# A copy moved into two number chains of VectorE, and gate matmuls cut to the chunks that are read

## The reference

```
# attention: 32 heads of 8, chunks of 32 tokens
gate = einsum('bshd,bnhd->bhsn', q, kmean)       # token against the mean key of each chunk
gate = where(future, NEG, gate); gate = where(self_blk, -NEG, gate)
sel  = top-4 chunks of each token and head
p    = softmax(where(sel & causal, q @ k.T * scale, NEG));  o = p @ v
rms  = rsqrt(mean(o * o) + EPS);  o = o * rms * o_norm_weight * sigmoid(g)
x    = layernorm(x + o @ Wo.T)
# experts: 2 shared, 16 routed with top-4 gates, 176 wide, relu
x    = layernorm(x + flat + shared + routed)
```

## Time and profile before

| | us |
|---|---|
| median of three runs | 1547.78 (1541.15 to 1549.93) |
| the profiled execution, its own time | 1541.77 |
| its span in the trace | 1539.7 |
| TensorE busy | 1373.1 (89%) |
| VectorE busy | 1170.6 (76%) |
| ScalarE busy | 845.4 (55%) |
| GpSimd busy | 550.0 (36%) |
| mean granted clock of TensorE | 0.958 of full |

### The profile page before, as it was taken

One profiled execution on the slowest core, in us unless ns is written; L12 is line 12 of the kernel. 1 busy time (PEld: TensorE's weight loads), 2 busy tenths in 40 slices (PEclk: granted clock), 3 DMA queues, 4 the chain that ended last, 5 costly groups with the idle time before them and its releaser, 6 DMA issues.

```text
span 1539.7 us, 29870 instructions
## 1 busy us (share of the span) xinstructions
PE 1373.1 (89%) x11220; PEld 756.7 (49%) x11220; DVE 1170.6 (76%) x2931; ACT 845.4 (55%) x1266; POOL 550.0 (36%) x638
## 2 busy tenths in 40 slices
PE   5587999999998899989999899989999899998697
PEld 3322565526653366534654266543664346552364
DVE  7993789867897688967898678976889668885534
ACT  5407663395625766286643956357662776438221
POOL 4204442254323442254322543235422443225143
PEclk8757999999999999999999999999999999999798
DMA  6001022200221021210122002210112102220031
GB/s 242 8 7 16 29 71 66 45 29 20 83 66 43 15 57 63 67 24 29 63 70 50 17 28 83 65 46 17 50 62 69 30 15 59 72 52 15 14 105 61
DMA packets 52212, 77.85 MB, mean 51 GB/s; under 512 B 6322, under 2 KB 26724, under 8 KB 51812
## 3 DMA queue, kind: packets, MB, share of 16 engines
q1 hardware_dynamic: 52068, 75.94, 16.8%
HBM read 67.00 MB, written 8.65 MB: 49 GB/s over the span
## 4 chain that ended last, share of the span: by engine, by line
PE 41%; DVE 36%; issue 8%; DVEq 5%; ACT 4%; POOL 4%; DMA 2%; SPq 0%; POOLq 0%
PE PS L570 10%; PE PS L558 7%; DVE CM L1340 6%; PE PS L713 5%; PE PS L487 4%; POOL hp L1045 4%; DVE hr L1141 3%; DVE ropeb L1360 3%; DVEq L1133 3%; PE PS L775 2%; DVE CM L1261 2%; ACT hp L849 2%; PE PS L401 2%; PE PS L723 2%; PE PS L504 2%
## 5 line engine op out<-in xcount | busy, mean ns | idle before, releaser
L1045 POOL TENSOR_TENSOR hp<-hr,hp 128x512 f16<-128x512 f32 (+1 forms) x200 | 237.2, 1186 | 601.7 <-ACT hp L849 569.7
L1340 DVE TENSOR_REDUCE CM<-PS 128x32 f32<-128x1024 f32 x320 | 378.2, 1220 | 29.0 <-PE PS L487 25.5
L570 PE MATMUL PS<-W,hp 128*128 128x256 f16 (+1 forms) x2400 | 314.1, 274 | 22.9 <-POOL hp L1045 20.6
L558 PE MATMUL PS<-x1T,W 128*128 128x512 f16 (+1 forms) x1200 | 307.9, 383 | 0.0
L570 PEld LDWEIGHTS PS<-W,hp 128*128 128x128 f16 (+1 forms) x2400 | 214.6, 98 | 109.9 <-POOL hp L1045 49.7
L849 ACT ACTIVATE hp<-hr 128x512 f16<-128x512 f32 (+1 forms) x178 | 112.6, 633 | 240.2 <-DVE hr L1141 225.3
L840 ACT ACTIVATE hr<-PS,CF 128x512 f32<-128x512 f32 (+1 forms) x200 | 136.8, 684 | 178.7 <-PE PS L558 173.4
L1141 DVE TENSOR_TENSOR hr<-hr,gB 128x512 f32<-128x512 f32 x176 | 128.9, 732 | 72.3 <-ACT hr L840 67.6
L989 ACT ACTIVATE UK<-PS 128x1024 f32<-128x1024 f32 x160 | 153.3, 1037 | 20.8 <-PE PS L504 19.4
L558 PEld LDWEIGHTS PS<-x1T,W 128*128 128x128 f16 (+1 forms) x1200 | 107.5, 99 | 109.3 <-issue 30.0
L989 ACT ACTIVATE UQ<-PS 128x1024 f32<-128x1024 f32 x160 | 154.1, 1036 | 12.4 <-PE PS L504 10.1
(11 more groups left out here) (157 smaller groups left out, 1963.5 us busy)
## 6 DMA issues: line engine op xcount, KB each, us to landing
gB<-gates SPq DMA_DIRECT2D x64, 256.0 KB, 3.3
gB<-gates SPq DMA_DIRECT2D x32, 224.0 KB, 2.9
gB<-gates SPq DMA_DIRECT2D x32, 192.0 KB, 2.8
gB<-gates SPq DMA_DIRECT2D x32, 160.0 KB, 2.6
xT<-in_xT SPq DMA_DIRECT2D x8, 512.0 KB, 4.0
qET<-rows SPq DMA_DIRECT2D x16, 256.0 KB, 5.2
v<-in_x SPq DMA_DIRECT2D x8, 512.0 KB, 4.0
gB<-gates SPq DMA_DIRECT2D x32, 128.0 KB, 2.9
```

Source lines behind the costliest of these rows:

```text
L558: mm = pe.matmul(PS[0:w, BK_H[c % 2], :], W1[:, a, k, bass.ds(f0, w)], x1T[:, e, k, :], start=(n == 0), stop=(n == 5))
L570: mm = pe.matmul(PS[:, BK_Y + j // 2, (j % 2) * D:(j % 2 + 1) * D], hp[0:w, slot, a, j * P:(j + 1) * P], W2[0:w, e, bass.ds(c, 1), :].rear ...
L1045: nc.gpsimd.tensor_tensor(hp[0:w, slot, 1, :], hr[0:w, slot, :], hp[0:w, slot, 0, :], ALU.subtract).then_inc(pool_hp, 1)
L1340: nc.vector.tensor_reduce(dst, src, AX.X, ALU.max).then_inc(dve_cm, 1)
```

## The change

Three edits. `chunk_gates` multiplies, for tile j, only the first 4(j + 1) chunks of each of the 16 heads of a half: 128, 192 and 256 columns. `copy_outputs(0)` is handed to `finish` and stands inside `layernorm`, between `newton` and the four scalings. In `two_groups`, `copy_outputs(2i + 2)` stands seven small instructions later, between `refine` and `newton`.

```diff
@@ chunk_gates
                 for j, bank in ((1, 3), (2, 0), (3, 1)):
+                    heads = lambda t: t.rearrange("p (h n) -> p h n", n=NCH)[:, :, 0:CPT * (j + 1)]
                     for m in range(KT):
-                        mm = pe.matmul(PS[:, bank, m * D:(m + 1) * D], qT[:, m, j * P:(j + 1) * P], KB[:, m, :],
+                        mm = pe.matmul(heads(PS[:, bank, m * D:(m + 1) * D]), qT[:, m, j * P:(j + 1) * P], heads(KB[:, m, :]),
                                        start=True, stop=True)
@@ layernorm
-            def layernorm(src, dst, done):
+            def layernorm(src, dst, done, between=None):
...
                 newton(NT)
+                if between is not None:
+                    between()
                 for j in range(NT):
@@ finish
-            def finish(m):
+            def finish(m, between=None):
...
-                layernorm(x1n, x1n, dve_out)
+                layernorm(x1n, x1n, dve_out, between)
@@ turn
-                if m is not None:
-                    finish(m)
                 def copy_outputs(g):
@@ two_groups
                     link(nc.vector.tensor_reduce(tok(ms), sq, AX.X, ALU.add))
-                    if not last:
-                        copy_outputs(i * 2 + 2)
                     link(nc.vector.scalar_tensor_tensor(out=tok(ms), in0=tok(rt), scalar=HD * 1e-6, in1=tok(ms),
                                                         op0=ALU.mult, op1=ALU.add))
                     root_guess(NT * 2 * HG)
                     refine(NT * 2 * HG)
+                    if not last:
+                        copy_outputs(i * 2 + 2)
                     newton(NT * 2 * HG)
@@ turn
-                copy_outputs(0)
+                if m is not None:
+                    finish(m, lambda: copy_outputs(0))
+                else:
+                    copy_outputs(0)
```

## The result

The changed kernel takes 1526.47 us (median of four runs, 1524.57 to 1527.54), the kernel before 1546.46 us in the same measurement (1541.15 to 1549.93). The ratio is 0.9874 with a 95% interval of 0.9852 to 0.9897: 1.3% faster, where 0.4% was forecast, and outside the stated range. The profiled execution took 1527.33 us with a span of 1525.3, against 1541.77 and 1539.7 before. So the two traces differ by 14.4 us and the medians by 20.

What follows compares the result with a forecast made beforehand. TensorE and VectorE handing work to each other were taken as the bound. 8.6 us gained, 1.2 lost and 0 for the gates made 7.4 us, scaled and shaded to 1541.4 us, 0.4% faster; range 1530 to 1551 us.

Steps and rivals of the forecast that it cites:

- part 2: Output norm, blocks 1 to 7: copying before the scalings removes TensorE's waits, 8.6 us gained (7 to 10.1).
- W: Even copies: time from the chain's first instruction (L1385) to the end of `refine`, put at 2.5 to 2.7 us.
- part 3: Even copies seven instructions later: odd waits go, even groups wait instead; 1.2 us slower in all.
- What bounds the stage: Hand-over between TensorE and VectorE: even copies bound by TensorE, odd ones by VectorE, with little slack.
- Part 1: Chunk gates: 0.66 us a block saved ahead of a wait that grows to about 1.6 us; 0 gained.
- 3.06 to 3.21 + W: Group loop: time from an odd group's transposes to the next even group's, 3.06 or 3.21 us plus W.
- 4.56 us of TensorE's own work: Group loop: TensorE's time from an even group to the odd one, with the odd copy no longer holding it.
- Rival (a): Even copies: chain meets fewer selects, W about 2.2 us, 9.1 us gained there; 1530 us by the median; chance 0.33.
- Rival (c): Output norm: ScalarE takes the wait over, the moved copy gains nothing; 1549 us by the median; chance 0.10.
- Rival (b): New waits at even groups and gate rows lower TensorE's clock, 1.46 us a fall; 1564 us; chance 0.12.
- The sum and the scale: Whole kernel: 7.4 us off the profiled 1541.77 gives 1534.4, scaled to the median 1547.78 as 1540.4 us.
- the shade: Whole kernel: 1 us added to the forecast time because W leans to the stalled side in the first pairs.

## Why the prediction was wrong

The direction of part 2 and the places of the waits were right. The step that failed is W, the time of the chain ahead of the even copy: it turned part 3 from a gain into a small loss. The steps in their order:

- What bounds the stage (TensorE's waits for odd copies, VectorE's for even ones): right. Each even copy had to pay for the odd one, and did.
- Part 1, nothing: right. 0.66 us was expected to be saved and 1.6 us of wait to stand there; 0.63 and 1.59 were found, and the gates alone gave 1.001.
- Part 2, "Sum 8.6 us": mechanism right, size low by a little, and not clear of the noise (the edit by itself measures 10.8 us, interval 7.4 to 14.0). The traces give 12.3 us in blocks 1 to 7. In blocks 2, 4, 5 and 6 the stretch fell by 1.57, 1.58, 1.88 and 1.57 us, which is the wait and 0.07 more. In block 7 the fall behind the wait went, too: 3.05 us, of which I had put 1.46 in the upper bound only. In blocks 1 and 3 the waits were 0.34 and 0.46 us and the stretch fell by 1.26 and 1.38. There the clock had fallen ahead of the transposes before, and in the changed kernel's trace it had not (rows below). That is luck of one execution: the norm edit alone has the same fall in two blocks, and there the stretch is 15.4 to 15.5 us, 0.4 to 0.6 under the 15.9 to 16.0 of before, much as the waits had said. So about 1.7 us of the 12.3 are due to two falls that did not come.

```profile
310.00:313.00 3.00, 3.00 (x20) 0.26 (x12) 2.32 (x10) 2.72 (x4) 1.22 (x3) 0.54 0.02 5
```

```profile
310.00:313.00 3.00, 3.00 (x44) 0.80 (x40) 2.36 (x9) 3.00 (x4) 1.68 (x4) 1.00 0.00 0
```

(The kernel before first, then the changed one; 0.54 and 1.00 are the granted clock.)

- Part 3, "W = 2.5", then "one more instruction is caught: 2.7": the step that failed. The formula 3.06 to 3.21 + W and the 4.56 us of TensorE's own work held within 0.1 us, but W was 2.43, 2.37 and 2.44 us in block 1, with two stalls and not three or four. In the second and third pair I took the beginning of GpSimd's three selects from the old trace, shifted, as 0.7 to 0.9 us behind the chain. It is 332.98 - 331.87 = 1.11 us in the second, because ScalarE's gap, which had stood in the odd groups, moved to the even ones, and GpSimd with it. And the instruction that starts just ahead of the first select is not held: in the row above the fifth starts at 332.92, 0.06 us ahead of the select, and takes its 0.19 us. In the first pair, where the place of the selects was right, the reckoning had the fifth start 0.10 us ahead of them and counted it as caught.
- The 2.5 itself is not the sum of its terms. Three instructions that wait for the ends of three selects are done no sooner than the selects, at 323.68 + 1.81 = 325.49, so W would be 325.49 - 322.52 = 3.0 us. That 2.5 lies near the measured 2.43 is luck: one stall too many, each counted too short. From group 1 to 7 it is 29.5 us for the forecast's 30.3: 0.8 us a block less, 0.66 of it by W, and 6 us over eight. In place of a loss of 1.2 us, the traces give a gain of 4.8 and the edit alone 7.4 (4.8 to 10.0).
- The rule on the lock, in the Trainium skill's "SBUF — State Buffer", section "SBUF: two separate sides": the instruction that ended `refine` had not been seen beside a select. Now it is, and takes 0.51 us (L1161 above) and 0.19 once the selects are small. By that rule it had to, and the trace agrees.
- Rival (a) had the right sign and nearly the size, by W = 2.2, though W was 2.4 and part of what it gained came from the norm; that its 1530 us lies near the measured time is partly luck. Rival (c) is out: the norm edit alone has a ratio of 0.9930, and ScalarE's 1.42 us gap of block 2 is gone. Rival (b) was seen with ten instructions ahead of the copy, at waits of 1.8 us, and not in the changed kernel.
- The sum and the scale: by the ratio, 0.4% was forecast and 1.3% measured, 13 us apart. By the edits alone 8.6 us of this lie in part 3, 2.2 in part 2 and 1 in the shade; the rest is within the noise of the ratios. The traces' difference of 14.4 us has 2.7 us against it from block 0 and the tail, where the change does nothing, and it is 17.1 without them. The 20 us of the medians are not shown to be more than that: the interval is 7 us wide, and by the later medians of the kernel before the difference is 16 to 19 us.

## What to carry to other kernels

A copy that hands a buffer from one engine to another should stand at the last place where it is still ready as its reader is: here behind five small instructions of a chain, where none or seven cost 1.6% and 1.1% of the kernel. Find that place by adding up the loop from one hand-over to the next on each engine, and look there for the instructions of GpSimd, for a short chain goes in steps of their length. When a change shifts one engine's gaps, the engines that follow it shift as well, so a stall read at the old place must be looked for again at the new one. And one wait is the price in its own execution only: where the clock had fallen ahead of it, the same late copy showed a wait of 0.34 us for 1.50, so read the stretch in several blocks and several traces before a difference is put down to the edit.

## What the runs showed of the hardware

- A VectorE instruction of 128x32 elements that meets a select or staging instruction of GpSimd ends a few hundredths of a microsecond after it. In block 1 of the changed kernel that makes 0.47 to 0.54 us for 0.19 at a select of 0.6 us, one stall per select when three follow each other. The copy out of PSUM never stretched: 0.68 or 0.69 us in all 64 of its rows in each of the twelve traces.
- Matmul records of 128, 192 and 256 float32 columns stream in proportion: 12 take 2.12 us where 12 of 256 columns take 2.75. Runs of 8 and of 12 columns in 16, in and out, cost nothing extra that shows.
- ScalarE's exponential of 128x1024 elements, shown at 1.04 us apiece, starts every 0.93 to 0.97 us where its rows have no gap (five in 4.63 or 4.83 us).
